# Eight weight buffers, straight-line experts, and text denominators in quarters, in a cross-attention and mixture-of-experts kernel

## The reference

```python
q = rms_norm(linear(x, q_w, q_b), norm_q_w)
img_x = attention(q, k_img, v_img)          # 257 image rows
txt_x = attention(q, k, v)                  # 1344 text rows
x = x + linear(txt_x + img_x, o_w, o_b)

h = layernorm(x)                            # 2048 rows
topk_idx, topk_w = router(h)                # 4 of 32 experts per row
Xp = h[slots_token].reshape(32, 80, 512)    # 80 slots per expert, later rows dropped
Y = (silu(Xp @ W_gate) * (Xp @ W_up)) @ W_down
out = zeros.at[slots_token].add(Y * slots_w)
x = x + out + (silu(h @ shared_gate.T) * (h @ shared_up.T)) @ shared_down.T
```

## Time and profile before

| | us |
|---|---|
| median of 3 runs | 1368.89 |
| lowest, highest | 1368.4, 1371.42 |
| profiled execution | 1375.18 |
| its span | 1373.3 |
| PE busy in it | 1226.1 |
| mean granted clock | 0.964 |

### The profile page before, as it was taken

How to read it: one execution, slowest core, us unless ns; L and a number is a source line. 1 busy time by engine, 2 the same in 40 slices (tenths; PEclk the granted TensorE clock), 3 DMA queues, 4 the chain that set the end, 5 groups by cost and what they waited for, 6 DMA issues and landing times. The chain is left out here.

```text
span 1373.3 us, 22309 instructions
## 1 busy us (share of the span) xinstructions
PE 1226.1 (89%) x9044; PEld 459.1 (33%) x9044; DVE 886.2 (65%) x1169; ACT 668.2 (49%) x910; POOL 184.1 (13%) x299
## 2 busy tenths in 40 slices
PE   4988999999899899989989998995798959989986
PEld 2542222444222245422224441221443423333332
DVE  6765878777587877767788766896667732222221
ACT  4546996345798534488853449882211101111111
POOL 0210000132000013200001320000200001333332
PEclk9999999999999999999999999997899989999997
DMA  7200000222000112200011122011620103989893
GB/s 276 88 23 17 2 2 10 83 70 70 24 1 1 58 41 64 93 1 1 2 69 32 62 77 94 9 55 44 257 100 3 39 1 108 308 281 321 278 289 76
DMA packets 38389, 117.82 MB, mean 86 GB/s; under 512 B 6544, under 2 KB 6800, under 8 KB 33040
## 3 DMA queue, kind: packets, MB, share of 16 engines
q1 hardware_dynamic: 33168, 105.60, 21.8%
q0 software_dynamic: 5120, 10.82, 3.7%
HBM read 95.67 MB, written 20.73 MB: 85 GB/s over the span
## 5 line engine op out<-in xcount | busy, mean ns | idle before, releaser
L567 ACT ACTIVATE work<-ps 128x1024 f32<-128x1024 f32 (+1 forms) x416 | 403.1, 1021 | 50.0 <-PE ps L1040 47.4
L1046 PE MATMUL ps<-work,vals 128*32 128x512 f32 (+2 forms) x1664 | 221.0, 604 | 1.1 <-ACT work L567 0.8
L863 PE MATMUL ps<-wts,work 128*128 128x512 f16 x864 | 203.1, 387 | 14.6 <-DVE work L596 14.6
L1040 PE MATMUL ps<-quer,keys 32*128 32x512 f16 x2496 | 171.8, 377 | 26.9 <-ACT work L567 9.3
L779 DVE TENSOR_TENSOR work<-work 128x2048 f32<-128x2048 f32 x64 | 146.6, 2291 | 5.9
L779 DVE TENSOR_TENSOR attn<-attn,work 128x2048 f32<-128x2048 f32 x64 | 146.6, 2290 | 5.3
L863 PE MATMUL ps<-wts,hl 128*128 128x512 f16 x480 | 116.6, 396 | 22.3 <-DVE hl L596 22.3
L863 PEld LDWEIGHTS ps<-wts,work 128*128 128x128 f16 x864 | 83.2, 99 | 115.1 <-DVE work L596 14.8
L1040 PEld LDWEIGHTS ps<-quer,keys 32*128 32x128 f16 x2496 | 46.2, 92 | 217.4 <-ACT work L567 192.0
L1816 PE MATMUL f_ps<-wring,xgt 128*80 128x512 f32 x256 | 116.5, 598 | 0.0
L1398 ACT ACTIVATE yf<-f_ps,wc 80x512 f32<-80x512 f32 x32 | 21.9, 683 | 174.7 <-PE f_ps L1831 168.2
(11 more groups left out here) (216 smaller groups left out, 1507.2 us busy)
## 6 DMA issues: line engine op xcount, KB each, us to landing
wring<-in_wx SPq DMA_DIRECT2D x32, 1536.0 KB, 8.1
raw<-in_ctx SPq DMA_DIRECT2D x52, 256.0 KB, 2.9
work<-in_x SPq DMA_DIRECT2D x4, 1024.0 KB, 5.4
table<-nums SPq DMA_DIRECT2D x16, 256.0 KB, 2.1
out<-x1s SPq DMA_DIRECT2D x16, 256.0 KB
work<-in_x SPq DMA_DIRECT2D x12, 256.0 KB, 4.3
x<-work SPq DMA_DIRECT2D x12, 256.0 KB, 2.0
x2t_rows<-nums SPq DMA_DIRECT2D x12, 256.0 KB, 2.4
```

The source lines that it names most:

```text
L567: act.activation(prob[0:rows, s % PROBS, 2 * half:2 * half + 2, :], ps[0:rows, 2 * pair:2 * pair + 2, :], ACT.Exp, scale=SCALE).then_inc(a ...
L863: mm = pe.matmul(out, lhs(a, c)[:, cols], wts[:, w, z, c * D:(c + 1) * D], start=(k == 0), stop=(k == len(steps) - 1))
L1040: mm = pe.matmul(ps[:, 2 * pair + h % 2, :], k[h * HD:(h + 1) * HD, :], q[h * HD:(h + 1) * HD, :], start=(e == 0), stop=(e == len(terms) - 1))
L1046: return pe.matmul(ps[h * HD:(h + 1) * HD, NUM, :], vals[a:z, ORDER[n], g * P + h * HD:g * P + (h + 1) * HD], prob[a:z, s % PROBS, h, :], ...
```

## The change

- Text denominators: four quarters of 128 columns, in steps 6 to 9, in place of two halves in steps 6 and 8.
- Eight weight buffers, each a tile of its own (`wring` is a list); gathers keep four (`GATHERS`). Six weights are loaded at the start of the second part, the seventh and eighth during the shared FFN, and 24 in the loop.
- The expert loops of PE, ACT, DVE and SP are written out in Python, without `Fori`; counts start at 0.
- ACT's order becomes: hidden copy of n, tanh of n+1, weighting of n. The hidden copy moves from DVE to ACT. `wc` goes; ACT reads the weight column from the gathered rows. Gathers no longer wait for `m_xt`, `m_w` and `f_gu`.
- The loads of x2t[0] and x2t[1] move from the end of the first part to the start of the second, and PE waits for them. x1 comes one sequence at a time into one buffer.
- Many tiles of the second part get new offsets. In the attention part, several semaphores that one engine only used to wait for itself become one per engine (`d_link`, `p_link`), with a wait at each former place.
- The expert products were f32 before and stay so.

The diff, cut to its core:

```diff
-RING = 4
+RING = 8
+GATHERS = 4
...
-        self.x2t = [at(f"x2t{i}", o * KB_, [P, QT, 2, NC, P], F16) for i, o in enumerate((8, 16, 48, 56))]
-        self.x1s = [at(f"x1s{i}", o * KB_, [P, 4, D], F32) for i, o in enumerate((74, 82, 90, 100))]
+        self.x2t = [at(f"x2t{i}", o * KB_, [P, QT, 2, NC, P], F16) for i, o in enumerate((48, 56, 64, 76))]
+        self.x1_last = at("x1_last", 8 * KB_, [P, QT, D], F32)
+        self.x1_block = at("x1_block", 190 * KB_, [P, QT, D], F32)
...
-        self.wc = [at(f"wc{i}", 198 * KB_ + 800 + 32 * i, [CAP, 1], F32) for i in range(RING)]
-        self.wring = at("wring", 132 * KB_, [P, RING, 3 * 2 * D], F32)
-        self.xg = [at(f"xg{i}", 8 * KB_ + 2176 * i, [CAP, TROW], F32) for i in range(RING)]
-        self.xgt = [at(f"xgt{i}", 17 * KB_ + 1280 * i, [P, NC, CAP], F32) for i in range(2)]
-        self.ht = [at(f"ht{i}", 20 * KB_ + 640 * i, [P, 2, CAP], F32) for i in range(2)]
-        self.eg = at("eg", 22 * KB_, [CAP, I], F32)
-        self.hh = at("hh", 23 * KB_, [CAP, I], F32)
-        self.yf = [at(f"yf{i}", (48 + 2 * i) * KB_, [CAP, D], F32) for i in range(2)]
+        self.wring = [at(f"wring{i}", o * KB_, [P, 3 * 2 * D], F32)
+                      for i, o in enumerate((132, 144, 156, 168, 84, 96, 64, 48))]
+        self.xg = [at(f"xg{i}", 116 * KB_ + 2176 * i, [CAP, TROW], F32) for i in range(GATHERS)]
+        self.xgt = [at(f"xgt{i}", 124 * KB_ + 512 + 1280 * i, [P, NC, CAP], F32) for i in range(2)]
+        self.ht = [at(f"ht{i}", 127 * KB_ + 640 * i, [P, 2, CAP], F32) for i in range(2)]
+        self.eg = at("eg", 128 * KB_ + 512, [CAP, I], F32)
+        self.hh = at("hh", 129 * KB_ + 512, [CAP, I], F32)
+        self.yf = [at(f"yf{i}", (108 + 2 * i) * KB_, [CAP, D], F32) for i in range(2)]
...
-                for t in range(2):
-                    sp.wait_ge(f_wlo, 3 * p + 2 + t)
-                    load_turned(t)
-                sp.wait_ge(s_xt, 32 * (p + 1))
...
-                        if g > 0 and n in (6, 8):
+                        if g > 0 and 6 <= n < 10:
                             if n == 6:
                                 pe.wait_ge(a_sum, added(bb, g - 1, ADDS - 1))
-                            at = 0 if n == 6 else HALF
-                            mm = text_part(g - 1, at, at + HALF)
-                            if n == 8:
+                            at = (n - 6) * P
+                            mm = text_part(g - 1, at, at + P)
+                            if n == 9:
...
+            def load_turned(b):
+                sp.dma_start(x2t[b][:, :, :, :, :].rearrange("p j a c k -> p j (a c k)"),
+                             x2_dram[b * L:(b + 1) * L, :].rearrange("(j p) n -> p j n", p=P)).then_inc(s_x2[min(b, 1)], 16)
+            def load_expert(n):
+                sp.dma_start(wring[n % RING][:, :], d["wx"][n]).then_inc(s_ring[n % RING], 16)
             sp.dma_start(x1t[:, :, :], d["x"][(B - 1) * L:B * L, :].rearrange("(j p) n -> p j n", p=P)).then_inc(s_xr, 16)
+            load_turned(0)
             sp.dma_start(rraw[:, :], d["rw"]).then_inc(s_r, 16)
             sp.dma_start(ebias[:, :], d["ebias"].partition_broadcast(P)).then_inc(s_r, 16)
-            sp.dma_start(x2t[2][:, :, :, :, :].rearrange("p j a c k -> p j (a c k)"),
-                         x2_dram[2 * L:3 * L, :].rearrange("(j p) n -> p j n", p=P)).then_inc(s_x2, 16)
-            for e in range(RING - 1):
-                sp.dma_start(wring[:, e, :], d["wx"][e]).then_inc(s_ring[e], 16)
+            load_turned(1)
+            load_turned(2)
+            for n in (0, 1, 2, 4, 5):
+                load_expert(n)
             sp.wait_ge(t_sel, NG)
-            sp.dma_start(wring[:, RING - 1, :], d["wx"][RING - 1]).then_inc(s_ring[RING - 1], 16)
+            load_expert(3)
             for j in range(QT):
                 sp.wait_ge(n_norm, j + 1)
                 sp.dma_start(table[(LB + j) * P:(LB + j + 1) * P, 0:D], xn[j]).then_inc(s_tab, 16)
-            for k in range(B - 1):
-                sp.dma_start(x1s[k][:, :, :], x1_dram[k * L:(k + 1) * L, :].rearrange("(j p) n -> p j n", p=P)).then_inc(
+            def load_rows(k):
+                upto(sp, s_o, 16 * QT * k)
+                sp.dma_start(x1b[:, :, :], x1_dram[k * L:(k + 1) * L, :].rearrange("(j p) n -> p j n", p=P)).then_inc(
                     s_xl, 16)
             def results(k):
                 for q in range(QT):
                     j = k * QT + q
                     sp.wait_ge(f_ac, j + 1)
-                    sp.dma_start(out[j * P:(j + 1) * P, :], x1s[k][:, q, :]).then_inc(s_o, 16)
+                    sp.dma_start(out[j * P:(j + 1) * P, :], (x1b if k < B - 1 else x1t)[:, q, :]).then_inc(s_o, 16)
+            load_rows(0)
             results(0)
+            load_rows(1)
             sp.wait_ge(e_wv, 1)
             sp.dma_start(table[0:T, D:TROW].rearrange("(j p) n -> p j n", p=P), rt[5][:, :, :]).then_inc(s_wt, 16)
             results(1)
+            load_rows(2)
+            sp.wait_ge(f_gu, 2 * NI)
+            load_expert(7)
+            sp.wait_ge(f_gu, 3 * NI)
+            load_expert(6)
+            results(2)
             sp.wait_ge(e_ar, 1)
             sp.dma_start(ia[:, :], arow_sb.rearrange("a (s e) -> a s e", e=E)).then_inc(s_ia, 16)
-            results(2)
             results(3)
-            with sp.Fori(0, E // RING - 1) as o:
-                for k in range(RING):
-                    sp.wait_ge(m_y, o * RING + k + 3)
-                    sp.dma_start(wring[:, k, :], d["wx"][bass.ds((o + 1) * RING + k, 1)].rearrange("a p n -> (a p) n")).then_inc(s_ring[k], 16)
+            for n in range(RING, E):
+                sp.wait_ge(m_y, n - RING + 1)
+                load_expert(n)
...
-            pool.wait_ge(f_gu, 2 * NI)
+            for n in range(GATHERS):
                 gather(n)
             pool.wait_ge(s_o, 16 * NT)
-            for n in range(1, E + 1):
-                if n > 1:
-                    pool.wait_ge(s_sc, (n - 1) * 16)
+            for n in range(E):
+                upto(pool, s_sc, 16 * n)
                 scatter(n)
-                if n + RING <= E:
-
-                    pool.wait_ge(m_xt, n)
-                    pool.wait_ge(m_w, n + 1)
-                    gather(n + RING)
+                if n + GATHERS < E:
+                    gather(n + GATHERS)
...
-            def expert(n, u):
-                act.wait_ge(m_gu, n)
-                act.wait_ge(m_t, n)
-                act.activation(eg[:, :], ps[0:CAP, 7 if u % 2 == 0 else 0, 0:I], ACT.Tanh, scale=0.5).then_inc(m_e, 1)
-                act.wait_ge(m_y, n + 2)
-                act.wait_ge(m_w, n + 1)
-                if not isinstance(n, int):
-                    act.wait_ge(s_sc, n * 16 - 32)
-                act.activation(yf[u % 2][:, :], ps[0:CAP, 2 + u % 2, :], ACT.Copy, scale=wc[u][:, 0:1]).then_inc(m_yf, 1)
-
-            for u in range(RING):
-                if u >= 2:
-                    act.wait_ge(s_sc, (u - 1) * 16)
-                expert(u + 1, u)
-            with act.Fori(1, E // RING) as o:
-                for u in range(RING):
-                    expert(act.snap(o * RING + u + 1), u)
+            def expert_tanh(n):
+                act.wait_ge(m_gu, n + 1)
+                upto(act, m_h, n)
+                act.activation(eg[:, :], ps[0:CAP, 7 if n % 2 == 0 else 0, 0:I], ACT.Tanh, scale=0.5).then_inc(m_e, 1)
+
+            def hidden_copy(n):
+                act.wait_ge(m_ht, n + 1)
+                upto(act, m_y, n - 1)
+                act.copy(ht[n % 2][:, :, :].rearrange("p c s -> p (c s)"), ps[:, 1, 0:2 * CAP]).then_inc(m_hc, 1)
+
+            def weighted(n):
+                act.wait_ge(m_y, n + 1)
+                upto(act, s_sc, 16 * (n - 1))
+                act.activation(yf[n % 2][:, :], ps[0:CAP, 2 + n % 2, :], ACT.Copy,
+                               scale=xg[n % GATHERS][:, D + n:D + n + 1]).then_inc(m_yf, 1)
+
+            expert_tanh(0)
+            for n in range(E):
+                hidden_copy(n)
+                if n + 1 < E:
+                    expert_tanh(n + 1)
+                weighted(n)
...
-                dve.wait_ge(s_xl, 16 * (B - 1))
+                if bk < B - 1:
+                    dve.wait_ge(s_xl, 16 * (bk + 1))
                 for q in range(4):
                     dve.wait_ge(f_dn, bk * 4 + q + 1)
-                    xq = x1s[bk][:, q, :]
+                    xq = (x1b if bk < B - 1 else x1t)[:, q, :]
...
-            def rows(n, u, count):
-                dve.wait_ge(m_xt, n)
-                dve.tensor_copy(xgt[u % 2][:, :, :].rearrange("p c s -> p (c s)"), ps[:, 6, 0:NC * CAP]).then_inc(m_xc, 1)
-                dve.wait_ge(s_g[u], count)
-                if not isinstance(n, int) or n > RING:
-                    dve.wait_ge(m_yf, n - RING + 2)
-                dve.tensor_copy(wc[u][:, :], xg[u][:, bass.ds(n - 1 + D, 1)]).then_inc(m_w, 1)
-            def hidden(n, u):
-                gu = ps[0:CAP, 7 if u % 2 == 0 else 0, :]
```

(63 more changed lines are left out.)

142 lines of the change are left out of this document (71 added, 71 removed).

## The result

The changed kernel takes 1365.66 us (median of 20 runs, 1359.08 to 1370.74), the kernel before 1370.82 in the same runs. The ratio is 0.9964 (0.9952 to 0.9977): 5.2 us faster. The profiled execution took 1366.32 us, span 1364.5. The first two fences are its busy times, from the page, and the stages of the earlier trace rows at the same times, from the windows (window, length, PE, PEld, DVE, ACT, POOL, clock, DMA share, GB/s).

The account below looks back on a forecast made before the run. ScalarE paces ordinary attention steps, PE the text steps, and the scatter chain the expert loop while weights load. Gains of 3.5 + 2.3 + 1.7 = 7.5 us take the 1368.9 us median to 1361.4, say 1361; range 1350 to 1370.

Parts of the forecast that it names:

- the quarters: Attention text steps: a quarter needs 1.96 us of PE against ScalarE's 1.95, so costs 0.01; 3.5 us gained in all.
- the ring: Expert loop: with eight weight buffers, four more steps at the end run without loads, 2.3 us gained (0 to 5.7).
- step 2: Attention: VectorE's sums set the end of fourth groups, so only 16 of 24 halves and 32 of 48 quarters count.
- step 4: Last expert: tanh ahead of the weighting removes PE's 2.03 us wait, less 0.32 for the hidden copy; 1.7 us gained.
- Rival 2: Attention: quarters cost as halves do, 0.24 us each; 3.8 us lost instead of 3.5 gained, 1368 us; chance 0.13.
- Unrolling: Expert loop: steps across loop ends already average 5.935 us, so writing the loops out gains nothing.
- rival 3: Expert loop: straight-line code fetched over saturated DMA, about 5 us per exposed fetch; 1371 us for two, 1376 for three; chance 0.12.
- Memory map: Second part's start and after: moved loads, offsets and merged semaphores cost zero, with 0 to 2 us for x2t[0].
- The named risk: Second part's start: PE's first gate_up waits for x2t[0], which may land late; delay beyond 1.67 us counts in full.
- The chain itself is unchanged: Expert loop: gathers keep four buffers and stay behind their scatters, so the larger ring gives no more than 2.3 us.
- Rival 1: Expert loop becomes bound by PE alone; another 12.4 us go at most, to 1349 us; chance 0.10.
- rival 4: Expert loop not relieved, only attention and tail gain: 1363.7 us; chance 0.62 together with the forecast.

Follow-up runs that it names:

- e1: The kernel before with text denominators in quarters and nothing else: 1365.74 us, ratio 0.9966 to the kernel before.
- e11: Changed kernel with 16 filling matmuls at each of three boundaries, bias additions held back until VectorE's weighting is done, and six gather buffers: 1349.91 us, ratio 0.986.
- e13: e11 with text denominators in two halves instead of four quarters: 1353.95 us, ratio 0.9895, mean 4.4 +- 3.1 us above e11.
- e3: Changed kernel with expert weights loaded only four experts ahead: 1362.7 us, ratio 0.9952 to the kernel before.
- e2: The kernel before with the expert loops of PE, ACT, DVE and SP written out and nothing else: 1368.58 us, ratio 0.9988.
- e5: Changed kernel with GpSimd's four bias additions at the second part's start held back until VectorE's weighting is done: 1365.29 us, ratio 0.9941.
- e7: Changed kernel with six gather buffers instead of four: 1358.79 us, ratio 0.9906 to the kernel before.
- e6: Changed kernel without the loop's 24 weight loads, experts 8 to 31 reusing weights of 0 to 7 (result partly wrong): 1354.02 us, ratio 0.9879.
- e12: e11 with expert weights loaded only four ahead: 1354.58 us, ratio 0.989, mean 4.3 +- 2.6 us above e11.
- e10: Changed kernel with 16 unread matmuls of 512 columns filling PE's idle stretch at each of three sequence boundaries: 1356.75 us, ratio 0.9914.

## Why the prediction was right, and where its steps were not

The forecast was 1361.4 against 1368.9, so 7.5 us less; 5.2 were measured. The steps on the quarters and on the ring had the mechanism right. That the sum came out near is in part luck: step 2 left out the fourth groups and did not look at what the last sequence gives back, step 4 was too large, and the start of the second part and the boundaries, which the sum doesn't hold (steps 6 and 8), move single executions by more than the whole gain.

1. **A quarter costs 0.01 us.** Right: steps of 1.97 and 1.98 against 1.96 forecast. Rival 2 is out. So is, for this form, the figure of the Trainium skill ("TensorE: Matmul & The Clock Gate", section "Back-to-back issue gap"): it made 0.65 us of the eight matmuls if each stood alone, and side by side they took 0.40.
2. **Only 16 of 24 halves are on the path.** Wrong. The step failed where it read VectorE's copy at the end of the fourth group as the end. Behind it the reciprocal waits for PE (1.02 us in the changed kernel, `<-PE ps L1086`), so PE's pace counts in the fourth group too: every sequence gained 1.17 us. In the last sequence much or all of it is then lost again; last score load to second part grew by 1.3 us in e1, 1.8 in the changed kernel and 0.7 in e11 against e13. Net 4.7 - 1.8 = 2.9 in the profile, 4.4 +- 3.1 by e13; forecast 3.5.
3. **Eight buffers, 2.3 us, by loads that end earlier.** The mechanism was right. With six gathers its size is 2.4 us in the loop of the profiles and 4.3 +- 2.6 in the means. With four gathers it isn't settled: e3's profile speaks for it (196.5 us from first to last scatter, against 190.4 to 193.8), its times don't.
4. **Last expert, 1.7 us.** Right in place, wrong in what it brings: 2.2 us at PE, but 1.2 at the end. The next thing late was the landing of the scatter before the last, which the step did not look at.
5. **Unrolling, nothing.** Right; rival 3 is out (e2, and no idle of that size in the changed kernel).
6. **Memory map, 0 to 2 us for x2t[0].** The named risk did not come: gate_up starts at 963.14. Another, which the step didn't look at, can cost 0 to 2.4 us: POOL's additions fall on VectorE's operations. That the overlap is the cost, e5's rows show. That the change brought it isn't shown: SP's load is issued 0.5 us earlier against PE, but e1, without that, shows a loss of 1.2 us at the same place.
7. **"The chain itself is unchanged, and that is why I expect no more from the larger ring."** True for the ring. But the chain was not the only way: e7 leaves scatters as slow as they were and gains 7.8 +- 4.3 us, 5 to 6 of them in the loop by the profiles, because PE's wait hung on gathers queued behind them.
8. **The boundaries, never priced.** Both kernels idle 4.03 us at each of three boundaries, and the clock falls. With halves and no filling they take 124.9 to 125.7 us in both profiles; with quarters 122.8 to 123.0 or 125.8 to 126.3, with nothing in the code that goes with the one or the other. Summed over the three, eight profiles of kernels with quarters and no filling give 368.7 to 378.7, mean 373.6, against 375.5. So the mean gains 2 us, less than eight such sums can tell from nothing, and single executions swing by 10.

The sum, by what was measured: quarters about 3, boundaries about 2 but not certain, last expert 1.2, start of the second part 0 to -2.4, and the ring and the order in the rest of the loop unsettled in this kernel. That covers 5.2 without saying exactly how it splits. Rival 1 (PE alone sets the loop) needs the loads gone, as in e6; rival 4 is not excluded for the kernel as changed: its 3.5 + 1.7 = 5.2 us is just what was measured.

## What to carry to other kernels

An idle stretch of the matmul engine costs more than its length when the granted clock falls behind it: look for the same instruction taking twice as long behind a wait, and try filling the wait with work that nobody reads. Where a prefetch sits in one queue behind a slow, ordered transfer, more buffers for the prefetch let the engines run past the transfer even though it becomes no faster. Small effects are best measured on a version from which the large random ones have been taken out: the ring's depth was lost in e3, whose 12 runs spread over 12.7 us, and visible in e12, with six runs over 6.0 beside six of e11 over 5.0.

## What the hardware showed that I had not expected

- A granted clock that falls again some 100 us after an idle stretch, late in dense projections (0.83 over 10 us at 575 us), in some executions and not in others, and now and then even when the stretch is filled (0.84 at 345 to 355 us in e10).
- 16 matmuls of no use at each of three boundaries made the kernel 8.1 +- 4.1 us faster.
- POOL's additions beside VectorE's operations on two SBUF tensors stretch these from 0.75 to as much as 1.84 us, and leave those with a PSUM operand at 0.68.
- With six gather buffers and waits of PE of at most 1.5 us, the granted clock stayed at 1.00 through the expert loop in four of four profiles; with four buffers it fell in seven of nine.
- An accumulating scatter of 80 rows lands in 3.9 us alone and in 5.8 beside weight loads; a gather in 3.2 and 5.0.
